# The first expert layer of a decoder kernel: the inner norm's variance taken from a Gram matrix, one product half as wide, and the weights' tail rows waited for by themselves

## The chip, the cores and the metric

The kernel runs on one core of one Trainium2 chip. Its time is the device time of one execution in microseconds. It is one large program of twelve stages (three parts for each of four decoder layers); the change lies almost wholly in the sixth, the mixture of experts of the second layer, which the code calls `l1f`. In the profile PE is TensorE (matmuls, PEld its weight loads), DVE is VectorE, ACT ScalarE, POOL GpSimd, and SP the engine that issues most DMAs.

## The reference, cut to what matters

2048 rows of 128 numbers pass a router, which picks 2 of 8 experts for each. Experts are of four kinds (0 to 3, twice). All share the way in (`up_W`, gelu) and out (`down_W`); kind 3 has nothing between.

```python
nx = _ln(x, ln_g, ln_b)
probs = softmax(nx @ router_w); idx = top_k(probs, 2); w = probs masked to idx, normalised
h1 = gelu(nx @ up_W[e] + up_b[e])                                         # 128 -> 512
s0 = gelu(_ln(h1 @ spec0_W + spec0_b, ln0_g, ln0_b))                      # kind 0
t1 = gelu(h1 @ spec1a_W + spec1a_b)                                       # kind 1: 512 -> 256
s1 = _ln(t1 @ spec1b_W + spec1b_b, ln1_g, ln1_b)                          #         256 -> 512
s2 = gelu(h1 @ spec2_W + spec2_b)                                         # kind 2
h2 = s0 / s1 / s2 / h1 by kind
out_e = h2 @ down_W[e] + down_b[e]
y = sum over the two experts of w * out_e, + x
```

For kind 1 the norm of `s1` is folded into the way out: `(t1 @ spec1b_W + b - mean) * rstd * g @ down_W` is `rstd` times a product of `t1` with a matrix that can be made once. What is still needed from `t1 @ spec1b_W + b` for each row is its variance.

## The kernel before, in words

**Dispatch.** Rows are sorted by expert into T = 39 tiles of 128 rows (some filled up), each of one expert. The class `Dispatch` finds on DVE and TensorE which expert each tile has (`found`) and which rows it holds (`known`). POOL gathers the rows of a tile by an indirect DMA (`gather`, L331), up to 8 tiles ahead, and scatters the results by another (`scatter`, L335). `step` is a counter by which DVE waits for its own earlier instructions.

**One tile for all kinds.** The loop over tiles has the same instructions for all experts; flags in `fl`, one column a tile, choose what counts. TensorE turns the gathered tile (`turn`), multiplies it up to 512 (`up`), makes the middle product of four chunks of 128 rows by 512 columns and a bias pass (`middle`, L1840 and L1841), turns the normed result (`turn_z`, L1850), makes the second product of two chunks of 512 columns and a bias (`second`, L1859 and L1860), and the way out (`down`, L1867). A matmul in f32 shows as two instructions in the profile. ACT applies gelu after `up` (`first`, L1958, into H1) and after `turn_z` (`activate`, L1967, into A2). DVE blends H1 and A2 by flag (`blend`, L2078 and L2080), takes the middle statistics and norms (`middle_stats`, `middle_norm`, L2085 to L2099, into Z), takes the statistics of the second product, only for its variance (`second_stats`, L2104 and L2108), and finishes the result (`result`, L2112 and L2117, into O). POOL turns each variance into a reciprocal root by two instructions (`root`, L1905 and L1907), the first time for the middle norm, the second time for the second.

**Order of the loop.** Each engine's queue is written out by hand. In round i TensorE does `turn_z(i-1)`, `middle(i)`, `up(i+1)`, `turn(i+2)`, `second(i-1)`, `down(i-1)`; DVE does `blend(i-1)`, `middle_stats(i)`, `middle_norm(i)`, `second_stats(i-1)`, `result(i-1)`; POOL does the middle root of i, the second root of i-1, the scatter of i-1 and, if a tile is left, the gather of tile i+7; ACT does `activate(i-1)`, `first(i+1)`, `take(i+2)`. In round 1 DVE also doubles X into R for the residual (L2131).

**Weights.** SP loads three pieces for each tile into a ring of four: WB (12 columns of vectors, 512 of `up`, 2048 of `middle`, 1024 of `second`), TB (tail rows: 512 columns of `down` or of its folded form, 128 of the folded bias, 128 of the bias) and RB (bias rows in three bf16 parts). All three count into one semaphore `loaded`, for which `up` waits. A slot is free when the result of its tile is made (`o_taken`).

**Ahead of the loop.** The fold of kind 1 is made on the chip: its inputs (`fold_pack`) are loaded into WB's last slot, ACT scales `down` by the gain (`gd`), TensorE and DVE centre it, TensorE multiplies by the transposed second matrix (`tail_ready`), ACT copies the result to TL, and SP writes it into the `tails` table in DRAM, before the tile loop's loads. Beside it the router runs on PE, ACT and DVE. POOL clears TL and RB by memsets early in the stage, while DVE norms the rows into NX (L2010).

## Time and profile before

| | us |
|---|---|
| median of 3 runs | 2170.95 |
| lowest, highest | 2170.48, 2173.26 |
| the profiled execution, its own time | 2172.46 |
| its span in the trace | 2170.7 |

| engine | busy us of the span | share |
|---|---|---|
| PE | 1771.8 | 82% |
| PEld | 1029.4 | 47% |
| DVE | 1427.0 | 66% |
| ACT | 1050.1 | 48% |
| POOL | 390.4 | 18% |

The page shows the span in 40 slices of 54.3 us. Stage `l1f` lies from the twelfth to the nineteenth, some 640 to 1040 us; there the DMA share is high (7 or 8 tenths), since weights come from DRAM for each tile, while in nearly all other slices it is 0. A row of the timeline gives start, duration, engine, line and operation, what is written from what, shapes, a count, and in brackets how long the engine stood idle before it and which instruction ended that. The shares are averages over stages with different limits, so the stage has to be read by itself.

### The profile page before, as it was taken

The numbers are of one execution on the slowest core, as the hardware profiler recorded it, in microseconds if no ns is written. First come the engines' busy times: TensorE is split into PE (matmuls) and PEld (weight loads), VectorE is DVE, ScalarE is ACT, GpSimd is POOL, SyncE is SP. The second block draws the span as 40 slices with busy tenths as digits, with TensorE's granted clock in tenths as the row PEclk, the third lists the DMA queues.
The fourth block names the chain that finished last, engine by engine and source line by source line (L and its number), as shares of the span: only waits on it lengthen the run. The fifth ranks groups of instructions, "written<-read, shape, count | busy, mean of one in ns | idle before, by whom it ended". The sixth has DMA issues, their size and how long they took to land. (4 is left out here: it accounts for less than half of the span.)

```text
span 2170.7 us, 33139 instructions
## 1 busy us (share of the span) xinstructions
PE 1771.8 (82%) x11797; PEld 1029.4 (47%) x11797; DVE 1427.0 (66%) x3243; ACT 1050.1 (48%) x2222; POOL 390.4 (18%) x574
## 2 busy tenths in 40 slices
PE   5769958999966999995778999994479999798682
PEld 3446642333344666663554444442244544465572
DVE  3436667888855655555546677675779999666434
ACT  3336635776723333331535655551367777465220
POOL 0010030000031544443120000001210000100373
PEclk8889978999977999997789999997689999899696
DMA  3000000000015788783000000000000000000474
GB/s 86 0 1 1 2 1 1 1 1 1 1 77 210 277 299 304 304 300 117 1 1 1 1 1 1 1 1 18 0 1 2 1 2 1 1 2 7 127 212 113
DMA packets 42700, 134.37 MB, mean 62 GB/s; under 512 B 7106, under 2 KB 22518, under 8 KB 37355
## 3 DMA queue, kind: packets, MB, share of 16 engines
q1 hardware_dynamic: 32363, 119.08, 15.6%
q0 software_dynamic: 4992, 10.23, 1.6%
q10 hardware_dynamic: 5184, 2.95, 0.5%
q8 instruction: 97, 1.59, 0.3%
q14 instruction: 64, 0.52, 0.1%
HBM read 123.14 MB, written 11.45 MB: 62 GB/s over the span
## 5 line engine op out<-in xcount | busy, mean ns | idle before, releaser
L160 POOL TENSOR_SCALAR rstd<-MV 128x2 f32<-128x2 f32 (+1 forms) x100 | 25.2, 252 | 1070.0 <-DVE MV L128 1064.2
L855 DVE TENSOR_REDUCE l1aM<-PS 128x2 f32<-128x1024 f32 x128 | 152.9, 1220 | 23.7 <-PE PS L611 21.7
L773 ACT ACTIVATE l1aE<-PS 128x512 f32<-128x512 f32 x256 | 140.8, 595 | 48.2 <-PE PS L640 46.7
L1840 PE MATMUL PS<-WB,H 128*128 128x512 f32 x312 | 143.5, 604 | 1.2 <-ACT H L1958 1.2
L773 ACT ACTIVATE l3aE<-PS 128x512 f32<-128x512 f32 (+3 forms) x256 | 102.5, 442 | 46.7 <-PE PS L644 43.8
L2652 ACT COPY PT<-PS 128x512 f32<-128x512 f32 x128 | 69.2, 589 | 94.7 <-PE PS L2563 94.5
L855 DVE TENSOR_REDUCE l3aM<-PS 128x2 f32<-128x256 f32 (+3 forms) x128 | 101.2, 818 | 19.4 <-PE PS L613 18.4
L2742 DVE TENSOR_REDUCE M<-PS 128x1 f32<-128x589 f32 x128 | 92.5, 764 | 26.5 <-PE PS L2552 26.0
L2658 ACT ACTIVATE E<-PS,M 128x589 f32<-128x589 f32 x128 | 95.9, 764 | 16.9 <-DVE M L2742 16.8
L1958 ACT ACTIVATE H<-PS,WB 128x128 f32<-128x128 f32 x156 | 44.6, 368 | 120.8 <-PE PS L1831 117.7
L883 DVE SCALAR_TENSOR_TENSOR l3aE<-l3aE,l3aLB 128x2048 f32<-128x2048 f32 (+1 forms) x64 | 94.9, 1482 | 2.6 <-ACT l3aE L773 2.6
L1967 ACT ACTIVATE A<-PS,WB 128x128 f32<-128x128 f32 x156 | 58.7, 457 | 77.4 <-PE PS L1850 77.4
L640 PE MATMUL PS<-l1aQS,l1aKS 128*128 128x512 bf16 x256 | 87.3, 387 | 4.5 <-ACT l1aE L773 3.7
L611 PE MATMUL PS<-l1aKS,l1aQS 128*128 128x512 bf16 x256 | 79.4, 393 | 13.7 <-DVE l1aKS L843 4.9
L1840 PEld LDWEIGHTS PS<-WB,H 128*128 128x128 f32 x312 | 57.3, 194 | 59.1 <-issue 57.6
L2580 PE MATMUL PS<-PT,Va 128*64 128x512 f32 x320 | 82.1, 611 | 0.8 <-ACT Q L2663 0.8
L2563 PEld LDWEIGHTS PS<-cols_const_sb,E 128*128 128x128 f32 x512 | 58.5, 145 | 50.2 <-DVE E L2762 30.0
L162 POOL TENSOR_TENSOR rstd<-rstd,mhalf 128x2 f32<-128x2 f32 (+1 forms) x100 | 76.1, 761 | 8.3
L1859 PE MATMUL PS<-WB,A 128*128 128x512 f32 x156 | 74.6, 601 | 1.7 <-ACT A L1967 1.7
L2552 PE MATMUL PS<-K,Q 64*128 64x512 f32 x256 | 75.7, 669 | 0.0
L2563 PE MATMUL PS<-cols_const_sb,E 128*128 128x128 f32 x512 | 71.7, 284 | 2.8 <-DVE E L2762 2.6
L640 PE MATMUL PS<-l3aQS,l3aKS 128*128 128x512 bf16 (+3 forms) x256 | 70.8, 305 | 3.3 <-ACT l3aE L773 1.7
(671 smaller groups left out, 4457.8 us busy)
## 6 DMA issues: line engine op xcount, KB each, us to landing
WB<-in_experts SPq DMA_DIRECT2D x39, 1798.0 KB
TB<-mixed_tails SPq DMA_DIRECT2D x39, 384.0 KB
WB<-in_experts SPq DMA_DIRECT2D x39, 384.0 KB, 3.6
WB<-in_fold SPq DMA_DIRECT2D x1, 1676.0 KB, 6.9
cols_l2x_sb<-in_cols_l2x SPq DMA_DIRECT2D x1, 1154.0 KB, 9.8
mixed_tails<-in_tails SPq DMA_DIRECT2D x1, 1152.0 KB, 9.4
mixed_rows<-R SPq DMA_DIRECT2D x4, 256.0 KB, 3.0
WB<-mixed_out SPq DMA_DIRECT2D x4, 256.0 KB, 5.7
```

Source lines behind the costliest of these rows:

```text
L162: g.tensor_tensor(out, out, self.mhalf[:, 0:out.shape[1]], ALU.pow).then_inc(done, 1)
L611: ins = mm(o, QS[:, pp, qt * P:(qt + 1) * P], keys(m)[:, pp, par, 0:kc], start=True, stop=not causal)
L640: ins = mm(o, keys(m)[:, pp, par, k0:k0 + kn], QS[:, pp, q0:S], start=True, stop=not (mask or causal))
L773: nc.scalar.activation(E[0:kn, home(m, kt) + j, q0:S], PS[0:kn, 4 + n % 2, q0:S], ACT.Exp, scale=SCALE).then_inc(exp_done, 1)
L855: v.tensor_reduce(M[:, m % 2, qt, 2 * hp:2 * hp + 2], PS[:, bank:bank + 2, 0:kc], AX, ALU.max, negate=True).then_inc(pair_free, 1)
L883: v.scalar_tensor_tensor(e, e, 1.0, LB[:, m % 2, :, kt * P:S], ALU.min, ALU.max).then_inc(clipped, 1)
L1840: mm(o, H1[:, i % 3, c * P:(c + 1) * P], mid_w(i, c), start=(c == 0), stop=False)
L2552: ins = mm(PS[:, at_ + 2 * par, :], Q[own, b % 2, pp, q], K[own, b % 2, pp, :], start=True, stop=True)
L2563: ins = nc.tensor.transpose(PS[:, at_ + 2 * par, t * P:(t + 1) * P], E[:, ring(x, par), e0:e0 + P], k.ident)
L2580: ins = mm(PS[64 * par:64 * par + 64, 6, :], Va[:, b % 2, t, h * DH:(h + 1) * DH], PT[:, n % 2, par, t, :], start=(t == 0), stop=(t == len ...
L2658: nc.scalar.activation(E[:, i, 0:NK], scores(s, par), ACT.Exp, bias=M[:, i:i + 1], accum_out=sums[:, i:i + 1]).then_inc(exp_done, 1)
L2742: ins = v.tensor_reduce(M[:, i:i + 1], scores(s, par), AX, ALU.max, negate=True)
```

## The change

The variance of `y = t1 @ W + b` over 512 columns is a quadratic form in `t1`: with the columns centred, `512 var = t1 G t1' + 2 c t1' + d`, where G = Wc Wc' is 256x256, c = Wc bc' and d = bc bc'. The new kernel does this:

- Ahead of the loop it centres W' and b (a matmul by ones, `w_summed`; ACT makes the negative means; POOL adds them, one instruction for each of the two experts, `w_centred`), makes G by TensorE (`squares`), c and d by TensorE (the cross products), and ACT writes them scaled into TL. TL is now a view of slots 2 and 3 of WB. The fold's inputs are loaded in the setup stage of the whole kernel, and stay in a tile of their own. `gd` moves into H2, `rep` into slot 1 of WB.
- A tail row grows by 769 columns: G, 2c/512, and d/512. WB loses its 1024 columns of `second`; RB and `bias_rows` lose theirs.
- In the loop `second` is a product of A2 with G: two chunks of 256 columns, no bias. DVE adds c (U), multiplies by the first 256 columns of the activated tile, sums, and adds d, in place of `second_stats`' two instructions. For that multiply ACT makes the unturned activation AT with one gelu of 256 columns.
- The order: `middle` is split; its first chunk now precedes `turn_z`. DVE's `blend` is split: its first instruction moves (`blend_first`) to behind `result`'s first (`result_base`) and ahead of its second.
- The tail table's rows count into semaphores of their own, `tailed`, for which `second` waits; `up` waits for `loaded` with 32 in place of 48.
- On SP the first weights are issued as soon as `found`; those of tile 1 wait for `tail_ready`; tail rows and the other tiles wait for the written tails.
- POOL's memsets come after all of NX and the two additions. On TensorE the dispatch list comes ahead of the fold's products, Gram and cross ahead of it.

```diff
-def experts_one(k, w, d, weights, tails, tails_made, bias_rows, bias_in, fold_pack, fold_at, rows, placed, gathered, scattered, ahead):
+def experts_one(k, w, d, weights, tails, tails_made, bias_rows, bias_in, fold, rows, placed, gathered, scattered, ahead):
...
-    VEC, UP, MID, SECOND = 12, 512, 2048, 1024
+    VEC, UP, MID, HALF = 12, 512, 2048, 256
+    GRAM, CROSS, CONST, TAIL = 6 * P, 6 * P + 2 * HALF, 6 * P + 3 * HALF, 6 * P + 3 * HALF + 1
...
-        WB = k.sb("WB", [P, RING, VEC + UP + MID + SECOND])
-        TB = k.sb("TB", [P, RING, 6 * P])
-        RB = k.sb("RB", [P, RING, 1024], BF16)
+        loaded, tailed, back = rings[0:RING], rings[RING:2 * RING], rings[2 * RING:]
+        WB = k.sb("WB", [P, RING, VEC + UP + MID])
+        TB = k.sb("TB", [P, RING, TAIL])
+        RB = k.sb("RB", [P, RING, S], BF16)
...
-        TL = k.sb("TL", [P, 2, 6 * P])
+        zy = k.sb("zy", [P, 32])
+        zys = k.sb("zys", [P, 3, 32], BF16)
+        TL = WB[:, 2:4, 0:TAIL]
+        AT = k.sb("AT", [P, 2, HALF])
+        U = k.sb("U", [P, 2, 2, HALF])
+        quad = k.sb("quad", [P, 2])
+        mean = k.sb("mean", [P, 2, HALF + 1])
         NX = k.R
-        fold = {n: WB[:, 3, lo:lo + m] for n, (lo, m) in fold_at.items()}
-        rep = WB[:, 2, 0:2 * 8 * P].rearrange("p (a c d) -> p a c d", a=2, c=8)
-        gd = WB[:, 2, 2 * 8 * P:3 * 8 * P].rearrange("p (c d) -> p c d", c=8)
+        rep = WB[:, 1, 0:2 * 8 * P].rearrange("p (a c d) -> p a c d", a=2, c=8)
+        gd = H2[:, :, :].rearrange("p a (c d) -> p (a c) d", d=P)
+        wT = fold["s1bT"].rearrange("p (j c f) -> p j c f", j=2, c=FC)
...
+            sp.wait_ge(found, 1)
+            sp.wait_ge(bias_out, 48)
+            sp.wait_ge(cleared, 2)
+
+            def weigh(i, e):
+                sp.dma_start(WB[:, i % RING, :], weights[bass.ds(e, P), :]).then_inc(loaded[i % RING], 16)
+                sp.dma_start(RB[0:3, i % RING, :], bias_rows[0:3, bass.ds(e * 4, S)]).then_inc(loaded[i % RING], 16)
+
+            def tail(i, e):
+                sp.dma_start(TB[:, i % RING, :], tails[bass.ds(e, P), :]).then_inc(tailed[i % RING], 16)
+
+            def chosen(i):
+                return sp.value_load(disp.expert_i[0:1, i:i + 1], min_val=0, max_val=7 * P)
+
+            weigh(0, chosen(0))
+            sp.wait_ge(tail_ready, 2)
+            weigh(1, chosen(1))
             for j in range(2):
                 sp.wait_ge(tail_made, j + 1)
                 sp.dma_start(tails[(4 * j + 1) * P:(4 * j + 2) * P, :], TL[:, j, :]).then_inc(tails_in, 16)
-            sp.wait_ge(found, 1)
-            for i in range(T):
-                e = sp.value_load(disp.expert_i[0:1, i:i + 1], min_val=0, max_val=7 * P)
-                if i == 2:
-                    sp.wait_ge(tail_ready, 2)
+            sp.wait_ge(tails_in, 80)
+            for i in range(2):
+                tail(i, chosen(i))
+            for i in range(2, T):
+                e = chosen(i)
                 if i >= RING:
                     sp.wait_ge(o_taken, i - RING + 1)
-                sp.dma_start(WB[:, i % RING, :], weights[bass.ds(e, P), :]).then_inc(loaded[i % RING], 16)
-                if i == 0:
-                    sp.wait_ge(tails_in, 80)
-                    sp.wait_ge(bias_out, 48)
-                    sp.wait_ge(cleared, 2)
-                sp.dma_start(TB[:, i % RING, :], tails[bass.ds(e, P), :]).then_inc(loaded[i % RING], 16)
-                sp.dma_start(RB[0:3, i % RING, :], bias_rows[0:3, bass.ds(e * 8, 1024)]).then_inc(loaded[i % RING], 16)
+                weigh(i, e)
+                tail(i, e)
...
+            for j in range(2):
+                for c in range(FC):
+                    ins = mm(PS[:, 5 + j, 0:HALF + 1], k.ones, wT[:, j, c, :], start=(c == 0), stop=(c == FC - 1))
+                ins.then_inc(w_summed, 1)
...
+            def squares(j):
+                pe.wait_ge(w_centred, j + 1)
+                for r in range(2):
+                    for c in range(FC):
+                        ins = mm(PS[:, 2 + 3 * j, r * HALF:(r + 1) * HALF], wT[:, j, c, r * P:(r + 1) * P], wT[:, j, c, 0:HALF],
+                                 start=(c == 0), stop=(c == FC - 1))
+                ins.then_inc(gram_ready, 1)
+
+            pe.wait_ge(centred, 2)
+            pe.wait_ge(mean_taken, 1)
+            squares(0)
             pe.wait_ge(marked, 1)
             disp.count_tensor(COUNTS, counted)
-            pe.wait_ge(centred, 2)
+            squares(1)
             pe.wait_ge(scaled, 2)
+            pe.wait_ge(affined, BT)
+            for j in range(2):
+                for c in range(FC):
+                    ins = mm(PS[:, j, 0:HALF + 1], rep[:, 0, j * FC + c, :], wT[:, j, c, :], start=(c == 0), stop=(c == FC - 1))
+            ins.then_inc(cross_ready, 1)
+            pe.wait_ge(lowered, 1)
+            disp.list_tensor(pe, LIST, spread, listed)
...
-            pe.wait_ge(lowered, 1)
-            disp.list_tensor(pe, LIST, spread, listed)
...
-            def middle(i):
+            def middle_start(i):
                 pe.wait_ge(hidden, FC * (i + 1))
                 if i >= 2:
                     pe.wait_ge(z_done, i - 1)
+                mm(PS[:, 1 + i % 2, :], H1[:, i % 3, 0:P], mid_w(i, 0), start=True, stop=False)
+
+            def middle_rest(i):
                 o = PS[:, 1 + i % 2, :]
-                for c in range(FC):
-                    mm(o, H1[:, i % 3, c * P:(c + 1) * P], mid_w(i, c), start=(c == 0), stop=False)
+                for c in range(1, FC):
+                    mm(o, H1[:, i % 3, c * P:(c + 1) * P], mid_w(i, c), start=False, stop=False)
                 mm(o, k.ones_b, RB[:, i % RING, 0:S], start=False, stop=True).then_inc(z_ready, 1)
...
             def second(i):
+                pe.wait_ge(tailed[i % RING], 16 * (i // RING + 1))
                 pe.wait_ge(activated, FC * (i + 1))
                 if i:
                     pe.wait_ge(y_stat, i)
-                o = PS[:, 4, :]
                 for c in range(2):
-                    mm(o, A2[:, i % 2, c * P:(c + 1) * P], second_w(i, c), start=(c == 0), stop=False)
-                mm(o, k.ones_b, RB[:, i % RING, S:2 * S], start=False, stop=True).then_inc(y_ready, 1)
+                    ins = mm(PS[:, 4, 0:HALF], A2[:, i % 2, c * P:(c + 1) * P], gram(i, c), start=(c == 0), stop=(c == 1))
+                ins.then_inc(y_ready, 1)
...
+            pool.wait_ge(nx_ready, NT * BT)
+            for j in range(2):
+                pool.wait_ge(mean_taken, j + 1)
+                g.tensor_tensor(wT[:, j], wT[:, j], mean[:, j:j + 1, :].broadcast_to([P, FC, HALF + 1]), ALU.add).then_inc(w_centred, 1)
+            g.memset(TL[:, :, 2 * P:4 * P], 0.0).then_inc(cleared, 1)
             g.memset(RB[:, :, :], 0.0).then_inc(cleared, 1)
...
             ins.then_inc(scaled, 1)
+            for j in range(2):
+                act.wait_ge(w_summed, j + 1)
+                nc.scalar.mul(mean[:, j, :], PS[:, 5 + j, 0:HALF + 1], -1.0 / 512).then_inc(mean_taken, 1)
             for b in range(BT):
                 act.wait_ge(turned_x, b + 1)
                 nc.scalar.activation(k.xt(b), PS[:, b % 2, :], ACT.Identity, bias=w["lnb"], scale=w["lng"]).then_inc(affined, 1)
             act.wait_ge(shifted, 1)
             nc.scalar.activation(pr[:, :, :], pr[:, :, :], ACT.Exp).then_inc(exped, 1)
-            for a, n in enumerate(("s1bb", "b1")):
-                for q in range(8):
-                    ins = nc.scalar.mul(rep[:, a, q, :], k.ones, fold[n][:, q:q + 1])
+            act.wait_ge(w_centred, 2)
+            for q in range(8):
+                nc.scalar.mul(rep[:, 0, q, :], k.ones, wT[:, q // FC, q % FC, HALF:HALF + 1])
+                ins = nc.scalar.mul(rep[:, 1, q, :], k.ones, fold["b1"][:, q:q + 1])
             ins.then_inc(scaled, 1)
+            for j in range(2):
+                act.wait_ge(gram_ready, j + 1)
+                nc.scalar.mul(TL[:, j, GRAM:GRAM + 2 * HALF], PS[:, 2 + 3 * j, :], 1.0 / 512)
             disp.spread_scalar(act, tiled, lowered)
+            act.wait_ge(cross_ready, 1)
+            for j in range(2):
+                nc.scalar.mul(TL[:, j, CROSS:CROSS + HALF], PS[:, j, 0:HALF], 2.0 / 512)
+                ins = nc.scalar.mul(TL[:, j, CONST:TAIL], PS[:, j, HALF:HALF + 1], 1.0 / 512)
+            ins.then_inc(cross_taken, 1)
...
             def activate(i):
+                act.wait_ge(z_done, i + 1)
+                if i >= 2:
+                    act.wait_ge(y_stat, i - 1)
+                nc.scalar.activation(AT[:, i % 2, :], Z[:, i % 2, 0:HALF], ACT.Gelu).then_inc(half_made, 1)
...
+            def blend_first(i):
+                dve.wait_ge(hidden, FC * (i + 1))
+                if i >= 2:
+                    dve.wait_ge(o_ready, i - 1)
+                v.tensor_scalar(H2[:, i % 2, :], H1[:, i % 3, :], fl[:, K3, i:i + 1], None, ALU.mult).then_inc(half_blended, 1)
+
             def blend(i):
                 dve.wait_ge(activated, FC * (i + 1))
-                if i >= 2:
-                    dve.wait_ge(o_ready, i - 1)
-                step(v.tensor_scalar(H2[:, i % 2, :], H1[:, i % 3, :], fl[:, K3, i:i + 1], None, ALU.mult))
-                step.wait()
+                dve.wait_ge(half_blended, i + 1)
                 v.scalar_tensor_tensor(H2[:, i % 2, :], A2[:, i % 2, :], fl[:, N3, i:i + 1], H2[:, i % 2, :], ALU.mult, ALU.add).then_inc(h_done, 1)
...
             def second_stats(i):
-                n = 2 + i % 2
+                n = i % 2
                 dve.wait_ge(y_ready, i + 1)
-                step(v.bn_stats(s6[:, n, :], PS[:, 4, :]))
+                step(v.tensor_tensor(U[:, n, 0, :], PS[:, 4, 0:HALF], TB[:, i % RING, CROSS:CROSS + HALF], ALU.add))
+                dve.wait_ge(half_made, i + 1)
+                step.wait()
+                step(v.tensor_tensor(U[:, n, 1, :], U[:, n, 0, :], AT[:, n, :], ALU.mult))
+                step.wait()
+                step(v.tensor_reduce(quad[:, n:n + 1], U[:, n, 1, :], AX, ALU.add))
                 step.wait()
                 if i >= 2:
                     dve.wait_ge(y_root, 2 * (i - 1))
-                v.bn_aggr(mv[:, n, :], s6[:, n, :]).then_inc(y_stat, 1)
+                v.tensor_tensor(mv[:, 2 + n, 1:2], quad[:, n:n + 1], TB[:, i % RING, CONST:TAIL], ALU.add).then_inc(y_stat, 1)
+
+            def result_base(i):
+                dve.wait_ge(o_ready, i + 1)
+                v.tensor_tensor(OB[:, i % 2, :], PS[:, 6, 0:P], TB[:, i % RING, 4 * P:5 * P], ALU.add).then_inc(based, 1)
 
             def result(i):
-                dve.wait_ge(o_ready, i + 1)
-                step(v.tensor_tensor(OB[:, i % 2, :], PS[:, 6, 0:P], TB[:, i % RING, 4 * P:5 * P], ALU.add))
-                step.wait()
+                dve.wait_ge(based, i + 1)
...
+                    result_base(i - 1)
+                if i < T:
+                    blend_first(i)
+                if i:
                     result(i - 1)
```

## Rows read from the trace of the kernel before

**Rows 1.** Windows: busy us and count of PE, PEld, DVE, ACT, POOL; PEclk, DMA share, GB/s.
```profile
692.00:696.00 4.00, 4.00 (x12) 1.96 (x11) 0.42 (x1) 0.00 (x0) 0.00 (x0) 0.65 0.98 381
724.00:764.00 40.00, 40.00 (x178) 24.23 (x177) 23.55 (x51) 15.43 (x47) 19.54 (x30) 1.00 0.82 304
```

**Rows 2.** Timeline of TensorE, one round in the middle of the loop.
```profile
826.00 3.60 PE L1840 MATMUL PS<-WB,H 128*128 128x512 f32 x8
...
830.66 1.88 PE L1859 MATMUL PS<-WB,A 128*128 128x512 f32 x4
832.38 0.38 PE L1860 MATMUL PS<-RB,ones_b 128*128 128x512 bf16 x1
832.59 1.05 PE L1867 MATMUL PS<-TB,H 128*128 128x128 f32 x8
...
833.92 3.60 PE L1840 MATMUL PS<-WB,H 128*128 128x512 f32 x8
```

**Rows 3.** Timeline of DVE, an early round that did not wait for TensorE.
```profile
713.85 0.81 DVE L2099 TENSOR_SCALAR Z<-PS,mz,rs 128x512 f32<-128x512 f32 x1 [1.06 <-POOL rs L1907]
714.57 0.69 DVE L2104 BATCH_NORM_STATS2 s<-PS 128x6 f32<-128x512 f32 x1
715.29 0.18 DVE L2108 BATCH_NORM_AGGREGATE mv<-s 128x2 f32<-128x6 f32 x1
...
716.66 0.35 DVE L2117 SCALAR_TENSOR_TENSOR O<-OB,rs,TB 128x128 f32<-128x128 f32 x1 [1.01 <-POOL rs L1907]
717.03 0.49 DVE L2078 TENSOR_SCALAR H<-H,flags 128x512 f32<-128x512 f32 x1
```

**Rows 4.** Timeline of POOL, same round, and its root for tile 38.
```profile
711.78 0.99 POOL L331 DMA_INDIRECT XG<-mixed_rows,l1f_of  x1 [0.30 <-issue]
712.81 0.35 POOL L1905 TENSOR_SCALAR rs<-mv,flags 128x1 f32<-128x1 f32 x1
...
715.58 0.34 POOL L1905 TENSOR_SCALAR rs<-mv,flags 128x1 f32<-128x1 f32 x1 [1.77 <-DVE mv L2108]
...
717.30 1.16 POOL L335 DMA_INDIRECT mixed_out<-O,l1f_to  x1 [0.75 <-DVE O L2117]
...
996.97 0.34 POOL L1905 TENSOR_SCALAR rs<-mv,flags 128x1 f32<-128x1 f32 x1 [2.23 <-DVE mv L2089]
```

**Rows 5.** DVE groups by form: busy us, mean ns, idle before.
```profile
L122 DVE TENSOR_TENSOR R<-Y,X 128x256 f32<-128x256 f32 x24 | 9.8, 408 | 0.3
...
L1458 DVE TENSOR_REDUCE Mp<-PS 128x1 f32<-128x256 f32 x4 | 1.7, 425 | 2.4 <-PE PS L1279 2.4
```

**Rows 6.** Timelines of DVE and POOL where their instructions overlap, three pairs.
```profile
708.24 2.28 DVE L2131 TENSOR_TENSOR R<-X 128x2048 f32<-128x2048 f32 x1
...
708.62 2.86 POOL L335 DMA_INDIRECT mixed_out<-O,l1f_to  x1 [0.76 <-DVE O L2117]
...
836.54 0.75 DVE L2080 SCALAR_TENSOR_TENSOR H<-A,flags,H 128x512 f32<-128x512 f32 x1
...
836.93 1.22 POOL L331 DMA_INDIRECT XG<-mixed_rows,l1f_of  x1 [0.30 <-issue]
...
1552.32 0.99 DVE L3067 TENSOR_SCALAR HT<-HALL,sc 128x1536 f32<-128x1536 f32 x1
...
1551.78 1.56 POOL L162 TENSOR_TENSOR rstd<-rstd,mhalf 128x2 f32<-128x2 f32 x1
```

**Rows 7.** L2010 (min/median/max ns), a POOL group by form, an issue (KB, us to landing).
```profile
L2010 DVE TENSOR_SCALAR R<-X,MV,rstd x16: 315/338/3680, 642.7 to 650.7; 128x128 f32<-128x128 f32 x16
...
L1086 POOL TENSOR_TENSOR l3xKS<-l3xKb,cols_l3x_sb 128x616 f32<-128x616 f32 x3 | 4.2, 1426 | 0.2 <-ACT l3xKb L1098 0.2
...
WB<-in_fold SPq DMA_DIRECT2D x1, 1676.0 KB, 6.9
```

**Rows 8.** Timeline of TensorE: the first tile's middle, the last tile's second product.
```profile
688.56 6.77 PE L1840 MATMUL PS<-WB,H 128*128 128x512 f32 x8 [1.23 <-ACT H L1958]
...
1001.20 3.06 PE L1859 MATMUL PS<-WB,A 128*128 128x512 f32 x4 [1.68 <-ACT A L1967]
```

More of the change, by code:

```diff
@@ L1876, in _ @@
                 if i < T:
-                    middle(i)
+                    middle_rest(i)
                 if i + 1 < T:
@@ L1925, in _ @@
             act.wait_ge(w["landed"], 16)
-            act.wait_ge(fold_in, 16)
+            act.wait_ge(fold["landed"], 16)
             for q in range(8):
@@ L3386, in _ @@
                     load(sp, W[n])
-                for late in (l1f, disp, l2f):
+                for late in (l1f, disp, l2f, fold1):
                     load(sp, late)
@@ L3477, in decoder_kernel @@
             placed = nc.dram_tensor("mixed_out", (2 * B * S + Dispatch.TILES * P, P), F32).ap()
[L3478 to L3479 removed]
+            tails = nc.dram_tensor("mixed_tails", dram["tails1"].shape, F32).ap()
+            bias_rows = nc.dram_tensor("mixed_biases", (3, 8 * S), BF16).ap()
             gathered, scattered = indirect("l1f")
[L3481 removed]
+            experts_one(k, l1f, disp, dram["experts1"], tails, dram["tails1"], bias_rows, dram["bias1"], fold1,
                         rows, placed, gathered, scattered, second_ahead)
@@ L3616, in mixed_experts @@
     per = lambda x: x.reshape(-1, P).T
-    weights, tails, biases = [], [], np.zeros((8, 1024))
+    weights, tails, biases = [], [], np.zeros((8, 512))
     for e in range(8):
         kind, j = e % 4, e // 4
-        mid, second, down = np.zeros((512, 512)), np.zeros((256, 512)), a[f + "down_W"][e]
+        mid, down = np.zeros((512, 512)), a[f + "down_W"][e]
         gain, shift = np.ones(512), np.zeros(512)
@@ L3623, in mixed_experts @@
             mid, gain, shift = a[f + "spec0_W"][j], a[f + "ln0_g"][j], a[f + "ln0_b"][j]
-            biases[e, :512] = a[f + "spec0_b"][j]
+            biases[e] = a[f + "spec0_b"][j]
         elif kind == 1:
-            mid[:, :256], second, shift[:256] = a[f + "spec1a_W"][j], a[f + "spec1b_W"][j], a[f + "spec1a_b"][j]
-            biases[e, 512:] = a[f + "spec1b_b"][j]
+            mid[:, :256], biases[e, :256] = a[f + "spec1a_W"][j], a[f + "spec1a_b"][j]
         elif kind == 2:
             mid, shift = a[f + "spec2_W"][j], a[f + "spec2_b"][j]
-        weights.append(np.concatenate([per(a[f + "up_b"][e]), per(gain), per(shift), a[f + "up_W"][e], chunks(mid), chunks(second)], 1))
-        tails.append(np.concatenate([chunks(down), np.zeros((P, P)), np.broadcast_to(a[f + "down_b"][e], (P, P))], 1))
+        weights.append(np.concatenate([per(a[f + "up_b"][e]), per(gain), per(shift), a[f + "up_W"][e], chunks(mid)], 1))
+        tails.append(np.concatenate([chunks(down), np.zeros((P, P)), np.broadcast_to(a[f + "down_b"][e], (P, P)), np.zeros((P, 769))], 1))
     kinds1 = (1, 5)
@@ L3634, in mixed_experts @@
     first_row[0] = a[f + "down_b"][[1, 5]]
-    fold = dict(s1bT=np.concatenate([chunks(a[f + "spec1b_W"][j].T) for j in range(2)], 1),
+    fold = dict(s1bT=np.concatenate([chunks(np.concatenate([a[f + "spec1b_W"][j].T, a[f + "spec1b_b"][j][:, None]], 1)) for j in range(2)], 1),
                 down=np.concatenate([chunks(a[f + "down_W"][e]) for e in kinds1], 1),
-                g1=per(a[f + "ln1_g"]), b1=per(a[f + "ln1_b"]), s1bb=per(a[f + "spec1b_b"]), downb=first_row.reshape(P, 2 * P))
-    return np.concatenate(weights), np.concatenate(tails), biases.reshape(P, 64), fold
+                g1=per(a[f + "ln1_g"]), b1=per(a[f + "ln1_b"]), downb=first_row.reshape(P, 2 * P))
+    return np.concatenate(weights), np.concatenate(tails), biases.reshape(P, 32), fold
 def kernel(**inputs):
@@ L3680, in lay_out @@
     places["biases"], row = put(biases)
-    places["fold1"], arrays["fold1"] = put(fold)
+    places["cols", "fold1"], arrays["cols_fold1"] = put(fold)
     for n in ("experts1", "tails1", "bias1"):
```

39 lines of the change are left out of this document (18 added, 21 removed).

## The prediction

> **What bounds the kernel now.** I read the page first, found the 39 expert tiles of stage l1f as its longest run of full TensorE, and then took the stage apart: stretches for load and clock, the TensorE timeline of one round, then DVE and POOL beside it, and last the rows in which those two overlap.
>
> In the middle of the loop TensorE is busy 40.00 of 40.00 us at a granted clock of 1.00, while DVE has 23.55, ACT 15.43 and POOL 19.54 us [rows 1]. One round takes 833.92 - 826.00 = 7.92 us [rows 2], all matmul. So TensorE bounds the loop, and every pass taken out of it looks like pure gain. But a second loop closes almost as tightly. Call R the start of the POOL square root for the first norm of a tile. In the only early round where nobody waited for TensorE, the chain from R is: Z on DVE at R+1.04, the second statistics +0.72, their aggregate +0.72, the result O +1.37 (the POOL root in between), the scatter +0.64, and behind the scatter, on POOL's own queue, the gather and only then the next R [rows 3, 4]. A normal scatter takes 1.06 (2.86 less the 1.80 it was held up, below), the gap to the gather is 711.78 - 711.48 = 0.30, the gather takes 0.99, the step to the next root 0.04 [rows 4, 6]. Sum: 1.04+0.72+0.72+1.37+0.64+1.06+0.30+0.99+0.04 = 6.88 us. The DVE-POOL loop has only 7.92 - 6.88 = 1.04 us of slack today. All its steps are serial: DVE does Z(n) before the statistics of n-1, POOL does scatter and gather of n-1 before the root of n+1.
>
> **TensorE's share of the change.** The second product goes from 512 to 256 columns: its four passes fall from 832.38 - 830.66 = 1.72 to 0.86, and the bias pass (832.59 - 832.38 = 0.21) goes [rows 2]. Bounds for the halved pass: 0.11 per pass less than half (nothing overhead) to none saved on the weight load; columns rule in these rows, so half. TensorE's round becomes 7.92 - 0.86 - 0.21 = 6.85 us. Splitting `middle` so that its first chunk precedes `turn_z` adds no instruction; it covers the wait for Z with 0.86 us.
>
> **DVE's share.** One 128x512 statistics (pitch 0.72) is replaced by add, multiply and reduce over 256 columns. Rows: a tensor_tensor of 256 takes 0.41, a reduce of 256 to 1 takes 0.42 [rows 5]; with 0.03 to 0.04 between dependent steps that is 0.45+0.45+0.455 = 1.355, so +0.63. The small add stands where the aggregate stood (bounds 0.16 to 0.23 by small ops; no difference taken). `result_base` and `blend_first` (0.29 and 0.49) fit into the 1.37 in which DVE waits for POOL: free on DVE itself. Only the second half of the old blend is left before the next statistics. DVE's own ring is then R to O 1.04+0.72+1.355+1.37 = 4.5 (4.8 with the stall below), +0.37 to the blend [rows 3], +0.7 to the statistics, +1.0 to the next R (714.57 to 715.58): 6.6 to 6.9, as long as TensorE's.
>
> **What moving the blends costs on POOL.** The rows show that the two engines block each other. A DVE tensor_tensor with both inputs in SBUF (708.24 to 710.52) held a scatter issued at 708.62: 2.86 us. A blend with two SBUF inputs ended at 837.29 and stretched a gather begun at 836.93 to 1.22, 0.24 over normal; both fit "nothing moves from 0.1 after the start until DVE is done". A DVE tensor_scalar SBUF to SBUF (1552.32 to 1553.31) that started in the middle of a POOL pow kept that pow until 1553.34: 1.56 [rows 6].
> - `blend` used to run 0.5 us later, behind the 0.49 multiply; only the blend with a tensor input is left, at O+0.37 to O+1.12, and the scatter starts at O+0.64. Held until O+1.12 from O+0.74: +0.38 (bounds 0 and 0.48).
> - `blend_first`, the same 128x512 tensor_scalar, now starts 0.41 after the small add and ends at 0.90, while POOL's root instructions stand at 0.29 to 0.63 and 0.71 to 1.26. The first ends at 0.93 instead, all behind shifts: +0.30 (bounds 0 and 0.49, its whole length).
>
> New ring: 6.88 + 0.63 + 0.38 + 0.30 = 8.19, less 0.02 for the shorter last step: 8.17 us, over TensorE's 6.85 and even over today's 7.92. Bounds: 7.51 with no collision, 8.5 with both at their upper ends. Here is my choice: the serial chain on POOL, not TensorE, sets the new round.
>
> The Trainium skill ("SBUF — State Buffer", Who interferes with whom) speaks both for and against: a tensor_scalar in a 2-port mode and GpSimd exclude each other, which agrees with the 1.56; but it says, as inferred, that a tensor_tensor does not stall descriptor generation. The 2.86 disagrees here. By the page the 0.38 would vanish; I follow the row.
>
> **Length of the loop.** From R of tile 2 (712.81) to R of tile 38 (996.97) [rows 4] today: 284.2 us. In the new kernel 30 of these 36 rounds carry a gather: 30 x 8.17 = 245.1. In the last 6 the gather and its gaps go (8.17 - 1.29 = 6.9; TensorE 6.85): 41.4. Sum 286.5: +2.3 us. The last tile loses half of 3.06 us of passes [rows 8] and the bias, and gains 0.63 of DVE: -1.0 (bounds -2 and +0.3).
>
> **Start of the stage.** Three things. (a) One of the sixteen NX instructions took 3.68 us instead of 0.34 [rows 7], beside the POOL memset of RB. The memsets now come after all of NX: NX is done 4 us sooner. But POOL then runs two additions of 1028 elements; at 1.43 us for 616 [rows 7] that is 2.4 us each, then the memsets, and now the DVE casts behind NX meet them, before the centring that the router's reduce stands behind. Router -2.4 to +1.5; I take +1. The new Gram and cross products (48 passes of 256) lie in TensorE's wait for DVE's routing and cost nothing; if the clock is low, up to 2. (b) The tail products now follow the list instead of preceding it, 68 passes of 0.11 to 0.23: about 8 to 9 us behind the list, where today TensorE idles until the first gather lands; the first tile comes out about 2 us later than now. Against this, TensorE comes warm: today the first middle took 6.77 us against 3.60 [rows 2, 8], so 3.2 come back. (c) The tails are 0.79 MB each instead of 0.39, and slots 2 and 3 of WB serve as their buffer, so WB(2) waits until weights 1 (1.32 MB) and both tails are written (2.9 MB at 381 GB/s [rows 1] is 7.6, plus latency 2), and TB(0), TB(1) and WB(2) are read (2.9 MB, 9.5): about 19 us after the tail is made. R of tile 2 comes to 714.7 by this chain, with the 2.28 us doubling still holding the first scatter: +2 (bounds -3 and +6). Waiting for `tailed` apart costs nothing: TB lands two rounds ahead, and 2.24 MB in 8.17 us is 274 GB/s, under today's 304 [rows 1]. The fold load moves to the setup stage, whose successors cover it for 600 us; today it takes 6.9 us [rows 7], the price without cover.
>
> **Sum.** +2.3 -1.0 +2.0 = +3.3 us. Made against the profiled execution, 2172.46 (span 2170.7 and 1.8 around it): 2175.8. The median of the runs shown is 1.5 lower: 2174.3, rounded 2174.5.
>
> **Rivals.**
> 1. TensorE keeps the bound, 6.85 a round. 39 x 1.07 = 42 us less, with the start's +1: 2133.5. For: it is full today. Against: the serial 6.88 + 0.63 already exceeds 6.85, with no collision at all. 5%.
> 2. The collisions are milder, 7.5 to 7.9 a round. With none: 30 x 0.66 = 20 less: 2155. With `blend_first` alone, which is what the skill's page gives for a tensor_tensor against descriptors: 30 x 0.38 = 11 less: 2163. For: each collision hangs on 0.1 to 0.4 us of alignment. 30%.
> 3. Slower: POOL's ring worse than I count, both root instructions caught by `blend_first` (0.49 instead of 0.30) and the multiply or a late blend catching the gather: 8.4 a round, 30 x 0.2 = 6 more, with the start at its +6: 2184. It decides from 8.25 a round on. 20%.
> 4. Forecast: ring 8.1 to 8.25, 45%, own range 2168 to 2181.
>
> A measurement of this kernel tells about 0.2% (4.3 us) from no change. Faster by more: 5% + 25% of rival 2 + 3% of the forecast: 0.33. Within: 5% of rival 2 and 22% of the forecast: 0.27. Slower: 20% and 20%: 0.40. Range 2154 to 2187: down to rival 2 without collisions, up past rival 3; TensorE's 2133 stays outside.
>
> **What would show it.** Right: TensorE's busy share in the middle of the loop falls from 1.00 to about 0.84, rounds of about 8.2 us; POOL without idle between scatter, gather and root; scatters of 1.4 us; the second root stretched; from tile 32 on rounds of 6.9. Wrong: rounds of 6.85 with TensorE full (rival 1); scatters of 1.07 (rival 2); R of tile 2 outside 710 to 719 (start). A granted clock below 1.00 in the loop, where TensorE now idles 1.3 us a round, would spoil all of it.

## The result and the profile after

| | before | changed kernel |
|---|---|---|
| median us (11 runs each, one chip) | 2171.55 | 2179.42 |
| lowest, highest | 2167.12, 2176.2 | 2172.29, 2184.96 |
| profiled execution, its span | 2172.46, 2170.7 | 2180.64, 2178.8 |

The ratio is 1.0036 with a 95% interval of 1.0024 to 1.0048: slower by 7.9 us. The forecast was 2174.5, slower, in a range of 2154 to 2187.

The loop first. Windows of the changed kernel, middle of the loop (busy us and count of PE, PEld, DVE, ACT, POOL; PEclk, DMA share, GB/s):

```profile
724.00:764.00 40.00, 34.61 (x168) 22.23 (x167) 23.96 (x61) 16.64 (x49) 21.46 (x31) 1.00 0.70 265
764.00:924.00 160.00, 139.39 (x671) 90.28 (x670) 93.98 (x238) 68.11 (x200) 86.99 (x119) 1.00 0.76 280
```

TensorE was full in [rows 1]; now it works 0.87 of the time, at a granted clock of still 1.00, and nothing else is full either. That is the picture of a serial ring over two engines. One round of it, on TensorE:

```profile
824.64 0.66 PE L1889 MATMUL PS<-cols_const_sb,Z 128*128 128x128 f32 x4 [1.03 <-DVE Z L2164]
825.13 2.74 PE L1879 MATMUL PS<-WB,H 128*128 128x512 f32 x6
827.71 0.38 PE L1880 MATMUL PS<-RB,ones_b 128*128 128x512 bf16 x1
827.93 1.05 PE L1867 MATMUL PS<-XGT,WB 128*128 128x128 f32 x8
...
828.93 1.03 PE L1898 MATMUL PS<-TB,A 128*128 128x256 f32 x4
829.80 1.05 PE L1906 MATMUL PS<-TB,H 128*128 128x128 f32 x8
830.69 1.02 PE L1874 MATMUL PS<-WB,H 128*128 128x512 f32 x2
832.75 0.66 PE L1889 MATMUL PS<-cols_const_sb,Z 128*128 128x128 f32 x4 [1.04 <-DVE Z L2164]
```

The second product (L1898) is half of what it was in [rows 2], the bias pass behind it is gone, and the first chunk of `middle` (L1874, two instructions) stands before `turn_z` (L1889), which still waits 1.03 us for Z. DVE in the same round:

```profile
823.78 0.81 DVE L2164 TENSOR_SCALAR Z<-PS,mz,rs 128x512 f32<-128x512 f32 x1 [2.25 <-POOL rs L1952]
824.50 0.41 DVE L2169 TENSOR_TENSOR U<-PS,TB 128x256 f32<-128x256 f32 x1
825.02 0.43 DVE L2172 TENSOR_TENSOR U<-U,AT 128x256 f32<-128x256 f32 x1
825.48 0.42 DVE L2174 TENSOR_REDUCE quad<-U 128x1 f32<-128x256 f32 x1
825.94 0.16 DVE L2178 TENSOR_TENSOR mv<-quad,TB 128x1 f32<-128x1 f32 x1
...
826.21 0.48 DVE L2139 TENSOR_SCALAR H<-H,flags 128x512 f32<-128x512 f32 x1
827.54 0.35 DVE L2189 SCALAR_TENSOR_TENSOR O<-OB,rs,TB 128x128 f32<-128x128 f32 x1 [0.85 <-issue]
827.81 0.75 DVE L2144 SCALAR_TENSOR_TENSOR H<-A,flags,H 128x512 f32<-128x512 f32 x1
```

And POOL:

```profile
826.20 0.62 POOL L1950 TENSOR_SCALAR rs<-mv,flags 128x1 f32<-128x1 f32 x1 [2.46 <-DVE mv L2178]
826.90 0.55 POOL L1952 TENSOR_TENSOR rs<-rs,mhalf 128x1 f32<-128x1 f32 x1
828.19 1.32 POOL L335 DMA_INDIRECT mixed_out<-O,l1f_to  x1 [0.73 <-DVE O L2189]
829.81 0.99 POOL L331 DMA_INDIRECT XG<-mixed_rows,l1f_of  x1 [0.30 <-issue]
830.82 0.38 POOL L1950 TENSOR_SCALAR rs<-mv,flags 128x1 f32<-128x1 f32 x1
```

Read the three together. The root (L1950) begins 0.02 us behind the gather and Z begins 1.06 behind that root; from Z the chain runs through the quadratic form, the second root, O and the scatter into the next gather. The first instruction of the second root takes 0.62 beside the multiply of 826.21, where [rows 4] have 0.34, and the scatter 1.32 beside the blend of 827.81, where 1.06 is normal. From R(2) = 725.54 to R(32) = 968.49 a round takes 8.10 us, and 6.80 from there to R(38) = 1009.28, where no gather is left. The whole loop from R(2) to R(38) takes 283.74 us; before it was 284.16.

So the loop did not make the kernel slower. The stage's start did. TensorE in the changed kernel, from the second tile's middle product to the first tile's second product:

```profile
705.41 0.38 PE L1880 MATMUL PS<-RB,ones_b 128*128 128x512 bf16 x1
713.69 2.08 PE L1867 MATMUL PS<-XGT,WB 128*128 128x128 f32 x8 [7.90 <-DMA RB<-mixed_biases]
...
715.77 1.82 PE L1898 MATMUL PS<-TB,A 128*128 128x256 f32 x4
```

The queue of SP ahead of it:

```profile
690.60 0.38 SPq L1749 DMA_DIRECT2D WB<-in_experts  x1
...
691.51 1.19 SPq L1763 DMA_DIRECT2D mixed_tails<-WB  x2
703.08 1.95 SPq L1753 DMA_DIRECT2D TB<-mixed_tails  x2
705.81 0.33 SPq L1749 DMA_DIRECT2D WB<-in_experts  x1
```

Both tails are written from 691.5 on; SP waits 9.5 us for their landing in the table, then reads them back and only then issues the weights of tile 2, since slots 2 and 3 of WB were the tails' buffer. TensorE stands still for 7.90 us and comes back at the lower clock (next view, windows of the same kernel): `up` takes 2.08 us and the second product 1.82, where the round above has 1.05 and 1.03.

```profile
713.00:717.00 4.00, 3.31 (x12) 3.10 (x13) 0.00 (x0) 1.20 (x5) 0.00 (x0) 0.50 1.00 419
```

The difference of the spans, 8.1 us, along the trace:

| stretch | before | after | difference |
|---|---|---|---|
| span's start to the stage's first DVE statistics | 638.01 | 642.26 | +4.25 |
| from there to R(2) | 74.80 | 83.28 | +8.5 |
| R(2) to R(38) | 284.16 | 283.74 | -0.4 |
| R(38) to the stage's last O | 9.87 | 8.50 | -1.4 |
| from there to the span's end | 1163.9 | 1161.0 | -2.8 |

The first and the last line lie in stages that the change does not touch (the last one but for the combining of the results at the stage's end, which it leaves as it was), except that a load more stands in the setup. Whether that load costs something was a question for the runs.

### The profile page after: what moved, and what is told of

Read it like the earlier page. It is cut to its first block and busy times, and to the rows that moved or that the text cites. A ratio compares the mean times of both kernels' runs of the same rounds, so it can differ in the third digit from the quotient of the medians.

```text
span 2178.8 us, 33477 instructions
## 1 busy us (share of the span) xinstructions
PE 1748.3 (80%) x11822; PEld 1030.6 (47%) x11822; DVE 1435.1 (66%) x3321; ACT 1068.6 (49%) x2269; POOL 411.6 (19%) x576
## 5 line engine op out<-in xcount | busy, mean ns | idle before, releaser
L1879 PE MATMUL PS<-WB,H 128*128 128x512 f32 x234 | 107.4, 595 | 0.0
L2164 DVE TENSOR_SCALAR Z<-PS,mz,rs 128x512 f32<-128x512 f32 x39 | 31.6, 810 | 76.3 <-POOL rs L1952 76.3
L611 PE MATMUL PS<-l3aKS,l3aQS 128*128 128x128 bf16 (+3 forms) x256 | 65.5, 310 | 9.8 <-DVE l3aM L855 6.5
L2839 DVE TENSOR_SCALAR E<-E,sums 128x589 f32<-128x589 f32 x128 | 67.6, 528 | 4.5
## 6 DMA issues: line engine op xcount, KB each, us to landing
mixed_tails<-in_tails SPq DMA_DIRECT2D x1, 2305.5 KB, 12.1
```

Source lines behind the costliest of these rows:

```text
L611: ins = mm(o, QS[:, pp, qt * P:(qt + 1) * P], keys(m)[:, pp, par, 0:kc], start=True, stop=not causal)
L1879: mm(o, H1[:, i % 3, c * P:(c + 1) * P], mid_w(i, c), start=False, stop=False)
```

## The experiments

All runs but the last two were made on one chip. The first four ran together, beside the kernel before at 2174.05 us (25 runs).

**Gather out of the ring.** POOL issues the gather behind the first root of the next tile, in its wait for the second statistics, instead of between the scatter and that root:

```
                     m = i - 1
-                    root(1, m, y_stat, y_root, K1, C1)
-                    pool.wait_ge(o_taken, m + 1)
-                    disp.scatter(O[:, m % RING, :], m)...
                     if m + XRING < T:
                         pool.wait_ge(x_turned, m + 1)
                         disp.gather(XG[:, m % XRING, :], m + XRING)...
+                    root(1, m, y_stat, y_root, K1, C1)
+                    pool.wait_ge(o_taken, m + 1)
+                    disp.scatter(O[:, m % RING, :], m)...
```

> The changed kernel with one edit: POOL issues the gather of tile i+7 behind the middle root, where it waited 2.5 us, and no longer behind the scatter. Theory A (the serial ring root, Z, quadratic form, root, result, scatter, gather on DVE and POOL sets the round of 8.10 us): the 1.29 us of the gather leave the ring, TensorE's 6.85 us binds, 30 rounds shorten by 1.25, total 37 us less than the changed kernel, about 2142. Rival B (rounds of 8.10 come from TensorE stalls on Z through the DVE work alone, or from weights arriving late): the round stays at 8.0 or more, total within 4 us of the changed kernel. Rival C (shorter rounds run into DMA: 2.24 MB in 6.85 us is 328 GB/s): rounds of 7.2 to 7.5, waits of up or second on a DMA.

Measured: 2140.2 us (2134.04 to 2143.67, 4 runs), ratio 0.9834 (0.9808 to 0.986). Windows and POOL of this run:

```profile
764.00:924.00 160.00, 160.00 (x796) 108.92 (x795) 113.44 (x281) 78.71 (x232) 103.42 (x140) 1.00 0.88 327
```

```profile
824.76 0.61 POOL L1950 TENSOR_SCALAR rs<-mv,flags 128x1 f32<-128x1 f32 x1 [1.23 <-DVE mv L2178]
825.45 0.56 POOL L1952 TENSOR_TENSOR rs<-rs,mhalf 128x1 f32<-128x1 f32 x1
826.75 1.31 POOL L335 DMA_INDIRECT mixed_out<-O,l1f_to  x1 [0.73 <-DVE O L2189]
828.16 0.34 POOL L1950 TENSOR_SCALAR rs<-mv,flags 128x1 f32<-128x1 f32 x1
828.57 0.56 POOL L1952 TENSOR_TENSOR rs<-rs,mhalf 128x1 f32<-128x1 f32 x1
829.33 1.04 POOL L331 DMA_INDIRECT XG<-mixed_rows,l1f_of  x1 [0.19 <-issue]
```

TensorE is full, 160.00 of 160.00, and a round takes 6.847 us from R(2) to R(32): the 6.85 of the prediction's TensorE term. Both collisions are still there (0.61, 1.31); they no longer lie in the bound. So the order of the instructions on POOL is what had kept the change's gain from showing, 37 us in the loop (246.45 for 283.74).

**The same order in the kernel before.** The same move, without the change.

> The kernel before with the gather moved behind the middle root as in e1. Theory A (before the change TensorE binds with 7.91 us a round, and the POOL ring of 6.9 has slack): nothing, within 2 us of before, rounds of 7.91. Rival B (POOL's ring already bound the kernel before): rounds shorter, total less by over 5 us.

Measured: 2174.86 us (10 runs), ratio 0.9997 (0.9978 to 1.0016), rounds of 7.89 us, TensorE 40.00 of 40.00. There the ring was not the bound, as the prediction had it, and the order alone is worth nothing that can be measured.

**Both halves of the blend behind O.** `blend_first` leaves its place beside the second root and is called at the head of `blend`, behind O:

```
                     result_base(i - 1)
-                if i < T:
-                    blend_first(i)
                 if i:
                     result(i - 1)
```

> The changed kernel with the blend in one piece again: its multiply moves back behind the result, next to the second half. Theory A (the blends block POOL: the moved multiply stretches the first instruction of the second root from 0.34 to 0.62, the second half stretches the scatter from 1.06 to 1.32): both go, since the multiply is done before the scatter asks and the scatter is under way before the second half; round 8.10 - 0.28 - 0.26 = 7.56, 16 us less over 30 rounds, 1 more in the last six, about 2164, though DVE gets 0.5 us more between two statistics. Rival B (no blocking, only DVE's own order counts): root and scatter keep 0.62 and 1.32, the round stays or grows, total same or a few us more.

Measured: 2166.45 us (10 runs), ratio 0.9951 (0.993 to 0.9972). POOL of this run:

```profile
829.04 0.34 POOL L1950 TENSOR_SCALAR rs<-mv,flags 128x1 f32<-128x1 f32 x1 [2.46 <-DVE mv L2179]
...
830.74 1.08 POOL L335 DMA_INDIRECT mixed_out<-O,l1f_to  x1 [0.73 <-DVE O L2190]
```

Its DVE:

```profile
830.10 0.35 DVE L2190 SCALAR_TENSOR_TENSOR O<-OB,rs,TB 128x128 f32<-128x128 f32 x1 [0.97 <-DVE OB L2183]
830.37 0.48 DVE L2139 TENSOR_SCALAR H<-H,flags 128x512 f32<-128x512 f32 x1
830.89 0.75 DVE L2145 SCALAR_TENSOR_TENSOR H<-A,flags,H 128x512 f32<-128x512 f32 x1
```

The root is back at 0.34 and the scatter at 1.08: 0.28 + 0.24 = 0.52 less, and the round is 7.59, 0.51 less. So the two collisions together are shown to cost 0.5 us a round; the one edit takes away both, and what each costs is read from the rows. The round of 7.59 is also what the change takes without them: over the 6.88 of the old ring by 0.7, which is the quadratic form.

Two details came out otherwise than expected. The multiply was not done before the scatter asked: it ends at 830.85, 0.11 us behind the scatter's start, which costs nothing here, but in two rounds it ended 0.34 and 0.35 behind it, and those scatters took 1.28 and 1.30. And the last six rounds, without a gather, did not get shorter but longer, 6.98 us for 6.80: there POOL waits 0.76 us for the statistics on DVE, which the moved multiply delays in DVE's own queue.

**A buffer of their own for the tails.** The tail rows are made in slot 3 of WB and in a tile that shares its memory with U, OB and O, which are first used later; so the weights of tile 2 can be loaded ahead.

```
-            weigh(0, chosen(0))
+            for i in (0, 2):
+                weigh(i, chosen(i))
...
-        TL = WB[:, 2:4, 0:TAIL]
+        TL = [WB[:, 3, 0:TAIL], late[:, 0:TAIL]]
```

> The changed kernel with the buffer of the second tail row moved out of WB into a tile shared with U, OB and O, so that the weights of tile 2 are loaded at once with those of tile 0; only slot 3 still waits for the written tails. Theory A (the start is a serial chain of DMAs: weights 1, two tail writes, two tail reads, weights 2, for which up(2) waits 7.9 us): up(2) waits for nothing, the second product of tile 0 waits for its tail row instead, root of tile 2 some 9 us sooner, total about 2170. Rival B (the start is late because of the router or the slow clock): less than 3 us.

Measured: 2174.25 us (2168.44 to 2176.14, 10 runs), ratio 1.0002 (0.9987 to 1.0017). TensorE of this run:

```profile
706.86 0.38 PE L1885 MATMUL PS<-RB,ones_b 128*128 128x512 bf16 x1
707.07 1.05 PE L1872 MATMUL PS<-XGT,WB 128*128 128x128 f32 x8
...
709.32 1.13 PE L1903 MATMUL PS<-TB,A 128*128 128x256 f32 x4 [1.08 <-DMA TB<-mixed_tails]
```

No pause before `up` of tile 2, full clock, 1.08 us for the tail rows instead. R(2) comes 74.52 us after the stage's start, as before the change (74.80), not 83.28; the rounds stay at 8.10. The forecast of about 2170 was too low: against the kernel before beside it the run is 5 to 7 us below the changed kernel (ratio 1.0002 for 1.0036 and 1.0025), where its trace has 8.8 less at the start. With the start mended, the change makes no difference that can be measured, so its loss was the start.

The next three ran together too, beside the kernel before at 2175.82 us (16 runs).

**Both together.** The gather behind the next tile's first root (the text below calls the two instructions of that root "the two roots"), and the tails' own buffer.

> The changed kernel with the gather moved behind the two roots and ahead of neither of them (as in the run e1_gather_first) and with the tail rows made in a buffer of their own (as in e3_tail_buffer). Theory A, the two costs lie at different places and add up: the rounds take 6.85 us, bound by TensorE, from R(2) on; R(2) comes 8.8 us earlier than in e1_gather_first against the start of the stage; the kernel takes 2140.2 - 8.0 = 2132 us. Rival: with full rounds the transfers are at their limit (DMA share 0.88 and 327 GB/s in e1_gather_first), and without the pause at the start the weights of some tile come late: rounds above 6.85 us and over 2136 us. Rival 2: TensorE's clock falls in some stretch of the now gapless loop: rounds of about 13 us in that stretch.

Measured: 2133.2 us (2127.43 to 2136.34, 4 runs), ratio 0.9798 (0.9777 to 0.9819). R(2) stands 73.94 us after the start of the stage, 9.1 earlier than with the gather alone; a round takes 6.88. The first rival was right in a corner, in its mechanism and not in its time: in TensorE's rows of this run the weights of tile 3 came late,

```profile
715.05 1.16 PE L1872 MATMUL PS<-XGT,WB 128*128 128x128 f32 x8 [1.67 <-DMA RB<-mixed_biases]
```

and the first two rounds took 7.3 us; then they run at 6.85 with 327 GB/s. The clock did not fall.

**The changed kernel once more.**

> The changed kernel once more, as it is, for a second profile and for its time beside the other two on one chip. Theory A (its start of stage of +4.25 us was luck): the stage begins somewhere from 638 to 644 us, R(2) comes 83.3 us after the stage's start as in its first profile within 0.5, the rounds take 8.10 us and the time is 1.003 to 1.005 of the kernel before. Theory B (the load in the setup): the stage begins at 642.3 us again, within 0.5.

Measured: 2180.29 us (10 runs), ratio 1.0025 (1.0009 to 1.0042). The stage begins at 641.58, R(2) comes 83.68 later, the rounds take 8.10. The loss is there again, in the same place, with a ratio a little under the expected 1.003; from the stage's start to its last O this trace has +7.3 us against the kernel before, the first +6.7.

**The load of cols_fold at the stage's start instead of in the setup.**

> The changed kernel with the load of cols_fold moved from the setup to the start of the stage, ahead of the stage's other loads on SP; nothing else differs. In the profile of the changed kernel the stage began 4.25 us later than in the profile of the kernel before. Theory A: that is the luck of one execution's clock stretches and has nothing to do with the load (the kernel before with its gather first, which has no such load, began its stage at +4.96 too). Then this kernel takes what the changed kernel takes within 2 us, and its stage begins anywhere from 638 to 644 us. Theory B: the load in the setup delays the first stages by about 4 us. Then the stage begins at 638.0 us as before, and the kernel is 3 to 4 us faster than the changed one.

Measured: 2182.79 us (7 runs), ratio 1.0033 (1.0021 to 1.0045), against 2180.29 of the changed kernel beside it. Neither theory had this: the stage began at 636.18, earlier than in any other trace, and then TensorE waited:

```profile
643.08 6.43 PE L1804 MATMUL PS<-cols_fold_sb,cols_const_sb 128*128 128x257 f32 x16 [7.62 <-DMA cols_fold_sb<-in_cols_fold]
```

R(2) came 89.82 us after the start, 6.5 more than with the load in the setup. The load does need cover, and the setup gives it. On the early part of the kernel this run decides nothing, since it changed two things at once. So that was measured by itself, on another, slower chip: the kernel before took 2196.39 us there (23 runs).

**The kernel before with an additional load in its setup.** 1245 KB into a tile that nothing reads.

```
+                sp.dma_start(fold_spare[:, :], dram["fold1"][:, 0:FOLD_SPARE], ...)
```

> The kernel before with one load more in its setup, at the place where the changed kernel loads cols_fold: 1245 KB (2432 of the 3273 columns, as many as fit) into a tile that nothing reads. The computation is that of the kernel before. Theory A (the load in the setup costs nothing, the late starts of the stage are luck): the same time as before within 0.15%, and a profile whose stage begins anywhere between 636 and 644 us, as those of the four kinds of setup so far did. Theory B (the load delays the first stages): 2 to 4 us slower than before (ratio 1.001 to 1.002), with the stage beginning at 641.6 us or later, as in all six profiles of kernels with the load there.

**The kernel before as it is, beside it.**

> The kernel before as it is, for a second profile of it. The two profiles of setups like its own, apart from the first one, began the stage at 636.2 and 643.0 us, its own at 638.0. Theory A (luck): somewhere from 636 to 644, with R(2) 74.8 us after the stage's start and R(38) 284.16 us later whatever the start is. Theory B: 638 or earlier.

Measured with the load: 2196.61 us (12 runs), ratio 1.0003 (0.9983 to 1.0023). As it is: 2200.98 us (10 runs), ratio to itself 1.0019 (0.9999 to 1.004); that is how far apart two samples of one kernel lie. The stage's first statistics, with the load:

```profile
644.03 0.87 DVE L2003 BATCH_NORM_STATS2 S<-X 128x6 f32<-128x128 f32 x4 [1.39 <-PEq L87]
```

without it:

```profile
644.07 0.87 DVE L2000 BATCH_NORM_STATS2 S<-X 128x6 f32<-128x128 f32 x4 [1.39 <-PEq L87]
```

The two traces are within 0.1 us of each other at this point and at every start of a stage ahead of it. The times alone would not decide: their interval (0.9983 to 1.0023) still holds the 1.001 to 1.002 of Theory B. The traces say more. Without the load the stage began at 636.2 (e5_fold_late), 638.0, 643.0 (e4_before_gather_first) and 644.1 us, with it between 641.6 and 644.3. What differs is the clock. Up to the stage's start the granted clock was at its lower level for 117.3 us in the trace that began at 636.2 and for 120.7 in that of 638.0; for 129.7 in the five that began from 641.6 to 643.0, one of them without the load; and for 133.1 in the four from 643.9 to 644.3, again one of them without it. So the +4.25 of the first two profiles is a difference of 9 us at the lower clock, which also comes without the load. Whether the load makes such a course of the clock more frequent is not shown: the seven traces with it all lie in the two late groups, the four without it in all of them. From the stage's start on, the last two traces repeat: R(2) after 74.2 and 74.3 us, R(38) another 284.15 and 284.16 us on.

## Why the prediction was right, and where it was off

**The bound moved to the ring: right.** Rounds of 8.10 us for 8.17, of 6.80 for 6.9 behind the last gather, TensorE at 0.87 for 0.84. Rival 1 was TensorE's 6.85; the run with the gather out of the ring has exactly that, so its figure was right and only its bound was wrong.

**The terms of the ring.** The quadratic form was +0.63 and is +0.72: from Z to the small add 825.94 - 823.78 = 2.16, for 715.29 - 713.85 = 1.44 in [rows 3]. The add is followed by the multiply after 0.52, not 0.45. The blend beside the scatter was +0.38 and is +0.26: the blend starts 0.27 behind O, not 0.37. `blend_first` beside the root was +0.30 and is +0.28. Sum 6.88 + 0.72 + 0.26 + 0.28 = 8.14, of which small steps give 0.04 back. Three terms were wrong by up to 0.12 and cancel. Had both collisions been absent (rival 2), 7.59 and not 7.51 would have come out.

The Trainium skill ("SBUF — State Buffer", Who interferes with whom) infers that a tensor_tensor does not stall descriptor generation. In the changed kernel a tensor_tensor with two inputs in SBUF held a scatter to 2.86 us again, as in [rows 6]:

```profile
720.97 2.29 DVE L2207 TENSOR_TENSOR R<-X 128x2048 f32<-128x2048 f32 x1
...
721.35 2.86 POOL L335 DMA_INDIRECT mixed_out<-O,l1f_to  x1 [0.76 <-DVE O L2189]
```

The blends, which are scalar_tensor_tensor, held it to 1.32 and 1.31; where no such instruction was running as it began it took 1.08. For these indirect DMAs, whose row numbers (`l1f_to`) lie in SBUF, the measurement decides against the sentence. Following the row [rows 6] put 30 x 0.38 = 11 us into the forecast, of which 30 x 0.26 = 8 were there.

**Length of the loop: +2.3 predicted, -0.4 measured.** 30 rounds at 0.07 less are 2.1 us, 6 at 0.1 less 0.6.

**The last tile: -1.0 predicted, not confirmed.** The first two traces have 9.87 and 8.50 us from R(38) to the last O, -1.4. But the 3.06 us of [rows 8] had been read where the granted clock was partly low (0.66 from 1001 to 1006 us). In the three other traces of kernels with the old arithmetic (the gather moved, the load added, and the kernel before again) the same product took 1.98 us and the stretch 8.55 to 8.57, and the changed kernel's second trace has 8.76.

**Start of the stage: +2.0 predicted, +8.5 measured.** This is the step that was mis-sized, beyond its own bound of +6. R(2) was to come at 714.7 and outside 710 to 719 the step would be wrong: it came at 725.54, or 721.3 less the 4.25 that the stage began late. The router (a) was harmless: the routing's last instruction (L327) stands 39.2 us after the stage's start, before 39.1. DVE pays beside POOL's additions what it saves in NX, as these rows of DVE

```profile
651.33 2.18 DVE L224 CAST l1f_ids_b<-cols_disp_sb 128x32 bf16<-128x32 f32 x1
...
653.51 4.35 DVE L2076 CAST zys<-zy 128x32 bf16<-128x32 f32 x1
```

and this one of POOL show:

```profile
651.22 4.40 POOL L1938 TENSOR_TENSOR cols_fold_sb<-cols_fold_sb,mean 128x1028 f32<-128x1028 f32 x2 [2.02 <-DVE R L2071]
```

Part (b) was right in its sign: the first middle took 2.07 + 3.28 = 5.35 us (L1874, L1879) instead of 6.77, so 1.4 of the 3.2 us came back, and the first tile's statistics stand 57.1 us after the stage's start, before 57.6. The chain (c) was the right chain with too short links. ACT's copies of the tail end at 690.97, that is 1.3 us later than the last product (L1851, 689.67), from which I counted; from there to the weights of tile 2 it took 713.69 - 690.97 = 22.7 us, not 19, because the tails were back after 12.1 (691.0 to 703.1) and not 9.6, and the three reads took 10.6 and not 9.5; and the pause of 7.90 us put TensorE at the lower clock, 1.03 + 0.79 = 1.8 us on `up` and the second product. Together 1.3 + 3.7 + 1.8 = 6.8, about the miss of 6.6; the prediction does not write out every link up to 714.7, so this division of the miss is argued and not shown. The clock is what I had not asked for: I counted the chain as if TensorE took up its work as it had left it. What is shown is the chain as a whole: the run with the tails' own buffer removes it and gets 8.8 us back at the start, as much as the whole loss.

**The fold load in the setup: nothing predicted, nothing found** (1.0003, and 644.03 for 644.07), with 6.5 us as its price without cover, where the prediction had 6.9 [rows 7].

**How much of "slower" was luck.** The bound was foreseen and tested. The sum was not so good: the loop was forecast to lose 2.3 us and lost nothing, the start to lose 2.0 and lost 8.5, and these two misses, -2.7 and +6.5, in part made up for each other. Had the start cost what was forecast, the kernel would have been about as fast as before; the run with the tails' own buffer, at 1.0002, shows as much. So that it came out slower is due to the term that was mis-sized.

**What stays open.** The stretch behind the stage's last O gave back 2.8 and 3.5 us in the two traces of the changed kernel. The change leaves those stages alone, and over the nine traces other than the last two this stretch took between 1155.5 and 1163.9 us, and 1163.9 and 1162.9 in the two of them without the change. It is not separated from chance. The load was tried with three quarters of its size, as there was no room for more.

## What to carry to other kernels

When the engine that is full gets less to do, first close the next ring by hand, instruction by instruction and over both queues; here it stood 1.04 us behind and took all of the gain. A queue instruction that nobody waits for soon (the gather) belongs behind those for which somebody waits: the same move was worth nothing that can be measured before the change and 37 us of the loop with it. And a borrowed buffer is a chain: count write, landing, read back and the next load at their measured durations, and add the clock that a pause of the engine costs.

## What had not been expected of the hardware

- In these traces a DVE instruction held a scatter when it was already running as the scatter began, and the hold ended with it. In the changed kernel the blend began 0.38 us ahead (827.81, 828.19), ended 0.37 behind the scatter's start, and the scatter took 1.32 for 1.06. The multiply, a tensor_scalar, did the same: in the kernel before, in one round each, it ended 0.22, 0.30 and 0.34 us behind the scatter's start, which took 1.16, 1.23 and 1.29. With the whole blend behind O the blend began 0.15 us after the scatter (830.89, 830.74), and the scatter took 1.08, the blend 0.75 as always.
- TensorE kept a granted clock of 1.00 through the loop with a pause of 1.03 us in each round of 8.10, and stood at 0.50 (1.2 GHz) when it took up its work after a pause of 7.90.
- Two executions on one chip, of kernels with and without a load of 1245 KB, ran within 0.1 us of each other for 644 us, while two executions on another chip, both of kernels without a fold load in the setup, reached that point 6.8 us apart (636.18 and 642.97), with 117.3 and 129.7 us at the lower clock on the way.
